# The products of the second layer's weights at the end of the first phase, and the eight experts written out with a semaphore for each load

## What is computed

```
x = x + xattn0(norm(x), ctx)          # 16 heads over 128 context tokens of width 192
n = norm(x)
logits = n @ w_switch + b_switch      # 8 experts
route  = argmax(softmax(logits))
pos    = rank of the token within its expert, over all 8192 tokens in order
keep   = pos < 512                    # capacity of an expert
y      = relu(buf @ w1 + b1) @ w2 + b2   # per expert, 512 rows, 256 -> 1024 -> 256
x = x + where(keep, y[slot], n) * gate
x = x + xattn1_ffn(norm(x), ctx)
# layer 1's cell, 6 nodes c, each with three incoming edges q, k, v
q = ew[c,0] * (node_q @ We[eq] + be[eq]); k, v alike
node[c] = act_w[c] * mha(q @ Wq[c], k @ Wk[c], v @ Wv[c]) @ Wo[c] + q
```

## Time and profile before

| | |
|---|---|
| median of 3 runs | 4303.83 us (4300.75 to 4309.98) |
| profiled execution | 4306.31 us |
| its span, first to last instruction | 4304.0 us |
| mean granted clock of the matmul engine | 0.978 of full speed |
| busy: PE, DVE, ACT, POOL | 94%, 58%, 61%, 41% |
| start, up to the first matmul | 16.2 us |
| first layer, up to the first load of the experts | 660.3 us |
| experts, up to the first load of the fuse block | 258.6 us |
| fuse block, up to the first load of the second layer | 72.3 us |
| second layer | 3296.6 us |

### The profile page before, as it was taken

The page is one execution under the profiler, slowest core; times in us unless marked ns, Lnnn a source line. Parts: engine busy times, 40 slices in busy tenths (PEclk is TensorE's granted clock), DMA queues, the critical chain, the costliest instruction groups (busy, mean ns, idle before and its releaser), DMA issues.

```text
span 4304.0 us, 101370 instructions
## 1 busy us (share of the span) xinstructions
PE 4065.9 (94%) x38496; PEld 3449.7 (80%) x38496; DVE 2511.5 (58%) x6253; ACT 2646.6 (61%) x11818; POOL 1754.8 (41%) x1864
## 2 busy tenths in 40 slices
PE   7999996986899999999999999999999999999997
PEld 6888884664788888888888888888888888888885
DVE  6878871013566666666666666666666566666553
ACT  7878871211566666666666666666666666666663
POOL 4556651001344444444444444444444444444332
PEclk9999997997999999999999999999999999999998
DMA  3222112332000000000000000000000000000000
GB/s 111 65 63 72 60 46 94 116 111 89 18 14 16 14 14 13 13 13 14 13 13 13 21 13 15 11 12 12 12 12 12 11 12 11 19 11 14 4 4 6
DMA packets 116244, 129.66 MB, mean 30 GB/s; under 512 B 11926, under 2 KB 110596, under 8 KB 115136
## 3 DMA queue, kind: packets, MB, share of 16 engines
q1 hardware_dynamic: 102016, 107.53, 7.8%
q0 software_dynamic: 6144, 8.43, 0.7%
q10 hardware_dynamic: 7616, 7.34, 0.5%
HBM read 89.68 MB, written 41.94 MB: 31 GB/s over the span
## 4 chain that ended last, share of the span: by engine, by line
PE 58%; DVE 8%; ACT 5%; POOL 3%; issue 1%; DMA 0%; SPq 0%; POOLq 0%; DVEq 0%
PE c_product L1262 26%; PE c_product L1273 12%; PE c_product L1313 8%; PE c_scores L1303 6%; ACT c_front_probs L1083 4%; PE c_product L1336 4%; DVE c_neg_max L1138 2%; DVE c_xn L1123 2%; PE c_product L1324 1%; DVE c_routed L1123 1%; DVE c_x L1148 1%; POOL c_rstd L1029 1%; ACT c_probs L1083 1%; POOL c_probs L1041 1%; POOL c_front_probs L1041 1%
## 5 line engine op out<-in xcount | busy, mean ns | idle before, releaser
L1083 ACT ACTIVATE c_probs<-c_scores,c_neg_max 128x128 f32<-128x128 f32 x3072 | 1082.0, 407 | 480.6 <-DVE c_neg_max L1138 480.6
L1041 POOL TENSOR_TENSOR c_probs<-c_probs,c_row_inv 128x512 f32<-128x512 f32 x768 | 790.4, 1041 | 1211.0 <-DVE c_row_inv L1141 1208.3
L1262 PE MATMUL c_product<-c_nodes,cell_w 128*128 128x256 f32 x4352 | 1057.1, 383 | 2.9 <-DVE c_nodes L1129 1.2
L1262 PEld LDWEIGHTS c_product<-c_nodes,cell_w 128*128 128x128 f32 x4352 | 803.8, 191 | 124.8 <-issue 19.5
L1138 DVE TENSOR_REDUCE c_neg_max<-c_scores 128x4 f32<-128x512 f32 x1024 | 635.3, 682 | 255.2 <-PE c_scores L1303 255.2
L1083 ACT ACTIVATION_READ_ACCUMULATOR c_probs<-c_scores,c_neg_max 128x1 f32 x3072 | 758.3, 247 | 0.0
L1089 ACT COPY c_probsT<-c_product 128x512 f32<-128x512 f32 x768 | 413.3, 613 | 440.3 <-PE c_product L1313 440.3
L1083 ACT ACTIVATE c_front_probs<-c_scores,c_neg_max 128x128 f32<-128x128 f32 x1024 | 358.3, 403 | 188.5 <-DVE c_neg_max L1138 188.5
L1273 PE MATMUL c_product<-cell_w,c_nodes 128*128 128x256 f32 x1792 | 435.4, 383 | 0.0
L1313 PE MATMUL c_product<-consts_sb,c_probs 128*128 128x128 f32 x3072 | 398.7, 276 | 15.5 <-POOL c_probs L1041 14.4
L1313 PEld LDWEIGHTS c_product<-consts_sb,c_probs 128*128 128x128 f32 x3072 | 350.8, 142 | 48.6 <-POOL c_probs L1041 20.5
(11 more groups left out here) (158 smaller groups left out, 6551.5 us busy)
## 6 DMA issues: line engine op xcount, KB each, us to landing
e_w<-in_L_ffn_w SPq DMA_DIRECT2D x16, 1024.0 KB, 8.3
a_x<-in_x SPq DMA_DIRECT2D x32, 256.0 KB, 3.4
a_ctxT<-in_ctx_pairsT SPq DMA_DIRECT2D x32, 256.0 KB, 3.4
x<-a_x SPq DMA_DIRECT2D x32, 256.0 KB, 2.1
xn<-a_xn SPq DMA_DIRECT2D x32, 256.0 KB, 2.2
c_routed<-xn SPq DMA_DIRECT2D x32, 256.0 KB, 2.8
c_x<-x SPq DMA_DIRECT2D x32, 256.0 KB, 3.1
c_ctxT<-in_ctx_pairsT SPq DMA_DIRECT2D x32, 256.0 KB, 2.6
```

The source lines that it names most:

```text
L1041: nc.gpsimd.tensor_tensor(e, e, rinv[:, i, r].unsqueeze(2).broadcast_to([P, 4, T]), ALU.mult).then_inc(norm_made, 1)
L1083: a = nc.scalar.activation(probs(n)[:, r, k], S[r][:, k], ACT.Exp, bias=nmax[:, i, r, k:k + 1], accum_out=rsum[:, i, r, k:k + 1])
L1262: i = T_.matmul(m[:, u], w[:, k, u * P:(u + 1) * P], src[:, k], start=n == 0, stop=n == last)
```

## The change

- **Fused products.** `phase_fuse` goes. In `phase_first_layer`, 18 `F` steps (products) and 18 `B` steps (biases) are put into the orders of the matmul and vector engines: `F0 F1 B0 B1` behind the last job's `L`, and `F2 F3 B2 B3 ... B17` behind the last `r.n`. They take the four product banks of the phase. On the vector engine `F0^ F1^` stand between the last `r.sh` and `r.oh`, `B0^ B1^` behind `r.oh`, the rest behind `r.n^`. SP loads the 12 plain matrices, the small vectors, the operands of the first three jobs and `w1` of expert 0 in iteration `j == 4`; the operands of job n from 3 on follow when `B(n-3)` is made. The scaling of the plain matrices moves to POOL, one node a period in periods 6 to 11, as `w.s`, ahead of `rs1`.
- **Start.** The block for the constants goes; ACT issues constants, wk, wq, the mask of the first four jobs, w_switch and b_switch, and SP the rest. Each has its own semaphore. `buf` is zeroed by 16 transfers of 256 KB in place of 4 of 1024 KB. The mask comes in pieces of four jobs.
- **Router.** `r.oh` now also adds up the one-hots of the group's tiles, one short chained step for each tile, in `before`; `r.n` is then two matmul instructions in place of 16 (for 8 tiles), and `r.n^` loses two steps.
- **Rows.** `ROW_RING` goes from 9 to 8.
- **Experts.** The loop is written out. Rows, w1 and w2 have their own semaphores; b1 and b2 of all experts are loaded once. `turn(e + 1)` stands between the hidden and the output products of expert e, into a second `rowsT`. `w1` of expert 0 is there already.

```diff
 FIRST_POOL_ORDER = """
-S0.n1:1 S0.n2:1 S0.n3:1 S1.n0:1 S1.n1:1 S1.n2:1 rs1:2 S1.n3:1 put:9 rs:-1 S0.n0:0
+S0.n1:1 S0.n2:1 S0.n3:1 S1.n0:1 S1.n1:1 S1.n2:1 w.s:6 rs1:2 S1.n3:1 put:9 rs:-1 S0.n0:0
 """
+FUSE_PE_PLACES = """
+L:0 F0 F1 B0 B1
+r.n:0 F2 F3 B2 B3 F4 F5 B4 B5 ... F16 F17 B16 B17
+"""
+FUSE_DVE_PLACES = """
+r.sh:0 F0^ F1^
+r.oh:0 B0^ B1^
+r.n^:0 F2^ F3^ B2^ B3^ ... B16^ B17^
+"""
...
+    if j == 4:
+        ... ew, aw, be, row5, and 12 plain matrices
+        sp.wait_ge(buf_zeroed, 16 * parts.shape[0])
+        for n in range(RING):
+            fuse_load(n)
+        sp.dma_start(w1_first[:], halves(io["L0_ffn_w1"][0])).then_inc(w1_in, 16)
...
+for n in range(RING, len(fused)):
+    if n == RING:
+        store(JOBS - 1)
+    sp.wait_ge(prod, n_prod[f"B{n - RING}", JOBS - 1])
+    fuse_load(n)
...
+elif n == "w.s":
+    for a, s in ((fw[:, c, EDGE], q), (fw[:, c, OUT], aw[:, c:c + 1])):
+        nc.gpsimd.tensor_scalar(a, a, s, None, ALU.mult)
+    i = nc.gpsimd.tensor_scalar(fb[:, c, EDGE], be[...], q, None, ALU.mult)
...
+elif n[0] == "F":
+    pe.wait_ge(job_in[r], 32 * (int(n[1:]) // RING + 1))
+    project(product(n, j), weT[:, r], we[:, r]).then_inc(prod, 1)
...
-V.tensor_tensor(oh[:, 0:w], over_t(i8[:]), over_e(route), ALU.is_equal).then_inc(hot, 1)
+chain(V.tensor_tensor(oh[:, 0:w], over_t(i8[:]), over_e(route), ALU.is_equal))
+for t in range(w):
+    k = V.tensor_tensor(before[:, t0 + t + 1], before[:, t0 + t], oh[:, t], ALU.add)
+    if t < w - 1:
+        chain(k)
+k.then_inc(hot, 1)
...
-for t in range(w):
-    T_.matmul(m[:, w * E:w * E + E], ones, oh[:, t], start=t == 0, stop=t == w - 1)
-T_.matmul(m[...], tri, oh[:, 0:w], start=True, stop=False)
-for t in range(w - 1):
-    i = T_.matmul(m[...], ones, oh[:, t:t + 1].broadcast_to(...), start=False, stop=t == w - 2)
-i.then_inc(prod, 1)
+T_.matmul(m, cst[:, C_TRI:C_TRI + P], oh[:, 0:t1 - t0], start=True, stop=False)
+T_.matmul(m, cst[:, C_ONE:C_ONE + P], before[:, t0:t1], start=False, stop=True).then_inc(prod, 1)
...
 # phase_experts, matmul engine
+turn(0)
+for e in range(E):
+    ... waits for w1_in and xT_made, hidden products
+    if e + 1 < E:
+        turn(e + 1)
+    ... wait for w2_in, output products
 # phase_experts, vector engine
+dve.wait_ge(b2_in, 16)
+rows_turned(0)
```

More of the change, by code:

```diff
@@ L104, in phase_first_layer @@
     W2 = PAIR * T
-    X_RING, ROW_RING, GROUP = 4, 9, 4
-    MASK_JOBS, SENDS = 4, 3
+    X_RING, ROW_RING, GROUP = 4, 8, 4
+    MASK_JOBS, SENDS, RING = 4, 3, 3
+    plan = cell_plan()
+    NE = io["L1_ffn_We"].shape[0]
+    SCALE = 1.0 / np.sqrt(D // CELL_HEADS)
+    fused = [(c, k, plan[c]["edge"][k]) for c in range(NODES) for k in (TO_Q, TO_K, TO_V)]
     PAIRS_OF_HEADS = D // 32
@@ L117, in masked, with with_fused @@
     def masked(order):
-        return [(n, j) for n, j in order if n != "mk" or j % MASK_JOBS == 0]
+        return [(n, j) for n, j in order if (n != "mk" or j % MASK_JOBS == 0) and (n != "w.s" or j < NODES)]
+    def with_fused(order, table):
+        order = list(order)
+        for line in table.strip().splitlines():
+            after, *pieces = line.split()
+            name, back = after.split(":")
+            i = order.index((name, JOBS - 1 - int(back))) + 1
+            order[i:i] = [(p, JOBS - 1) for p in pieces]
+        return order
     on_pe, on_dve, on_act, on_pool = (masked(routed(unfold(t, JOBS))) for t in
                                       (FIRST_PE_ORDER, FIRST_DVE_ORDER, FIRST_ACT_ORDER, FIRST_POOL_ORDER))
+    on_pe, on_dve = with_fused(on_pe, FUSE_PE_PLACES), with_fused(on_dve, FUSE_DVE_PLACES)
     def is_turn(n):
@@ new lines, in _ @@
+            for e in range(E):
+                s = e % 2
+                if e >= 1:
+                    pe.wait_ge(w1_in[s], 16 * ((e + 1) // 2 if s else e // 2))
+                pe.wait_ge(xT_made, 2 * e + 2)
+                for c in range(HC):
+                    if e * HC + c >= HBANKS:
+                        pe.wait_ge(hid_made, e * HC + c - HBANKS + 1)
+                    b = HB[c % HBANKS]
+                    for u in range(2):
+                        i = nc.tensor.matmul(b[:], w1t[s][:, u, c * P:(c + 1) * P], xT[:, s, u], start=u == 0, stop=u == 1)
+                    i.then_inc(hid, 1)
+                if e + 1 < E:
+                    turn(e + 1)
+                pe.wait_ge(w2_in[s], 16 * (e // 2 + 1))
+                for q in range(YB):
+                    if e >= 1:
+                        pe.wait_ge(y_made, YB * (e - 1) + q + 1)
+                    for n in range(2):
+                        r = (2 * q + n) * P
+                        for c in range(HC):
+                            if q == 0 and n == 0:
+                                pe.wait_ge(hid_made, e * HC + c + 1)
+                            i = nc.tensor.matmul(Y[q][:, n], hT[:, c, r:r + P], w2t[:, s, c], start=c == 0, stop=c == HC - 1)
+                    i.then_inc(out, 1)
```

401 lines of the change are left out of this document (180 added, 221 removed).

## The result

The changed kernel takes 4277.88 us in the median of five runs (4268.57 to 4282.35); the kernel before, run beside it, 4303.83 (4300.75 to 4309.98, five runs). The ratio is 0.9932, 95% interval 0.9916 to 0.9948: faster by some 0.7%, where 1.2% was forecast. 4277.88 lies outside the range, 10 us above its upper end. The profiled execution took 4278.62 us, its span is 4276.8.

A forecast was written before the change was run, and what follows sets the result against it. The prediction took PE, busy 603 of 637 us in the first layer, as the bound. Experts' first load +30.2 (start, POOL, router and row), experts -11, fuse block -72.3: -53.1 from 4304.0 gives 4250.9, median 4251; range 4240 to 4268.

The forecast's parts named there:

- Fuse block, -72.3: Block between experts and second layer: its whole 72.3 us would go, DVE's 8 us of scaling at its end included.
- Experts, -11: Expert loop: a period falls from 30.3 to 28.7 us with copies under the output products, seven times -1.6.
- Start, -6.4: Kernel start: fewer bytes ahead of the first statistics, which move from 16.87 to 10.5 us; gain 6.4 us.
- Transfers in iteration 4, 0: SP's 24 transfers (5.7 MB) at about 63 us: covered by a period and a half of lead; price 0, +5 at most.
- Row, +38.8 from the last logits to the experts' first load: Row of fused products before the experts: 61.8 us, with sixteen jobs at 2.62 and seven load waits of 1.1 us.
- Plain matrices on POOL, +10, ends +7 and +17: Scaling in periods 6 to 11: 0.7 us each on POOL, 1.6 us a period on the path, +10 us.
- Router, -12.2, ends -4 and -19: First layer's counts: shorter count -3.1, additions +1.6, two steps fewer -0.35; -1.85 in each full group, -12.2 us together.
- Experts' entry, 0: Entry to the experts: DVE waits for b2 before its first copy, as many bytes lie ahead; 0, ends -2 and +3.
- Second layer, 0: Second layer: its orders are untouched, so it was carried over at its old length, 3297.
- First layer gives back: Rival, chance 0.20: scaling costs 2.7 us a period, longer PE waits drop its clock, routing gains only -4; 4259 to 4272.
- Row at half clock: Rival, chance 0.06: PE's 1.1 us waits in the row keep its clock at 0.50, 16 jobs cost 5.2 each; 4281.
- Gap stays: Rival, chance 0.08: 6 unexplained us between the last scatter's landing and the experts' first load stand behind the row; 4257.

The follow-up runs named there:

- the version with all edits: Changed kernel with scaling on DVE, late additions, row F B F B, late b2 wait, and first scaled copies behind the one-hot: 4230.82 us, ratio 0.9831.

## Why the prediction was wrong

It was right in direction and in most of its terms; the span came out 26 us above 4250.9. Two steps failed by some 10 us each, the price of a scaling on POOL and the gain of the router; a third, the clock behind the last count, by 3. Term by term, from the ledger:

- *Fuse block, -72.3*: right. *Experts, -11*: -11.8 for the seven later periods and the first together (245.0 without the block before, 233.2 after). Right.
- *Start, -6.4*: the first statistics stand at 10.32 (forecast 10.5) where they stood at 16.87; job 6 is reached 6.2 us earlier. Right, though in the other kernels with this start job 6 is reached 2.6 to 6.3 us earlier. The case in which the start brings only 2.9 us did not come.
- *Transfers in iteration 4, 0*: right; the periods of jobs 3 to 6 are 17.9, 17.3 and 17.3 us before and after.
- *Row, +38.8 from the last logits to the experts' first load* (61.8 against 23.0): measured +42.1. The head, 8.5 + 1.7 + 0.7 = 10.9, took 10.7 from the last logits to F2. What was mis-sized is the term behind it, sixteen jobs at 2.62: the first pair, F2 F3 B2 B3, took 7.8 us (675.73 to 683.54) in place of 5.2. The granted clock was 0.50 from 665 to 670 and 1.00 from 671 to 674, but behind the wait for the count it was 0.50 again from 675 to 680, and F2 F3 took 6.27 us for eight matmul instructions that take 3.9 at full clock. The forecast let the low clock end with the first four steps: 2.6 us. The seven waits were priced at 1.1 us and took 1.13, 0.79, 0.77, 0.97, 0.72, 0.81 and 1.53, 1.0 us less in all; with the 0.27 us that each costs besides, the other seven pairs took 45.4 us in place of 44.4. Pairs took 6.2 to 6.6 us, where 6.3 was said.
- *Plain matrices on POOL, +10, ends +7 and +17*: this is the step that failed. The scaling was bounded by the nearest rows, 0.52 for a memset and 1.26 for an addition, with 0.7 taken because only one tensor is read. It took 1.57, outside both ends, and above the 1.3 that the prediction named as a sign of being wrong. The price per instruction was more than twice too low, and the upper end of the bound was an assumption: that the two-tensor form is the dearest. The cost is 18 to 22 us by the ledger and by the run without it, so the error is 8 to 12 us. The path was right: `rs1` and the last normalisation, and PE waiting for POOL. One for one was right only as a sum, and by luck: of POOL's 20.6 us, 13.5 became idle time of PE, and 6.2 came from the lower clock, a term that the sum did not have.
- *Router, -12.2, ends -4 and -19*: the second step that failed. The additions' +1.6 was right, PE's wait grew by just that. What the sum put at nothing is the clock: the lower one behind the longer wait stands in the text only as what makes the -4 end. PE's busy time fell by 1.9 us a count in place of 3.1. Measured: -0.3 a count outside the scaling periods, and in all -2 (the ledger: jobs 6 to the last logits +17.7, less the scaling's 19.7) to -5 (the run with the old router), so an error of 7 to 10 us. The additions late gave 20.6 us a count period, 2.1 less than the changed kernel's mean of 22.7.
- *Experts' entry, 0*: measured -0.7. The wait for b2 was named with the right place in the queue, yet priced at nothing because as many bytes as before lay ahead. The comparison was right; but the 6 us could be had.
- *Second layer, 0*: +3.9 in the profiled executions. In the ten other kernels with the same second layer it is -3 to +5 against before. Nothing tells it from spread.

The Trainium skill, GPSIMD Engine Reference, section Engine selection, calls one-input elementwise work on this engine roughly line-rate. The rows here don't bear that out for a scaling by a scalar column: 1.57 us where the two-input product of the same shape took 1.04.

Of the rivals, *First layer gives back*, at 0.20, had the right mechanism, the lost clock among it, and both of its parts came true (4259 to 4272 by its prices, with 1.26 a scaling). With 1.57 it gives 2 x 0.31 x 6 = 4 us more, and with the row's 3.4 its upper end is 4279. *Row at half clock* was wrong: the clock is 1.00 from 683.5 on in spite of waits of 1 us. *Gap stays* and the far side were not seen.

Two things stay open. At the head of the row the signals of B0 and B1 reach DVE and SP 2 to 5 us behind the last record of their matmuls (in the version with all edits the last record ends at 642.9 and the signals come at 645.3 and 647.5). The changed kernel doesn't show this: SP's load behind B0 goes out at 672.24, while B1's records are still running. PE's ends are modelled, and whether it was still at work there or its signals were late, no run tells. And the head at half clock was not tried against a version that keeps PE busy before it.

## What to carry to other kernels

Before work is moved to another engine, find a row of that very form of instruction on that engine; a neighbouring form is no bound, and two forms of one computation can differ by half. Where an engine's order is written out by hand, ask of every new step whose signal is queued behind it: additions that nobody waits for soon stood ahead of a reciprocal that POOL, and behind it PE, waited for, and a wait for a bias stood ahead of copies that did not need it; either cost 6 to 9 us and was moved by one step in the order. In a ring of loads, spread the steps that free a slot evenly between those that need one: the same jobs and transfers in pairs cost 9 us more than one by one. Where the matmul engine is the bottleneck, price a longer wait with the clock behind it: here the clock took 6 us of the 20 that the scaling cost, and 1.2 of the 3.1 us that each count had saved.

## What the runs showed of the hardware

- On GpSimd a 128x512 f32 TENSOR_SCALAR with a scalar column took 1.56 to 1.57 us, a TENSOR_TENSOR with the same column broadcast 1.04, a memset 0.52. On VectorE the TENSOR_SCALAR took 0.48 to 0.52.
- Twelve matmul records that take 1.53 us at full clock took 2.12 us behind a wait of 1.53, 2.36 behind one of 1.66 and 2.82 behind one of 3.14. Behind the last of these the granted clock was 0.50 from 316 to 322. A wait of 1.5 us did not always cost clock: in the period at 303.55 of the kernel before, it was 1.00 and the twelve took 1.53.
- Waits of 0.7 to 1.5 us every 6.2 to 6.6 us left the granted clock at 1.00 in the row (683.5 to 730.2).
